# Where the causal mask is added to the query-major scores: matmul, or VectorE together with the row maximum

## The reference

```
def _L1_attn_ref(x, Wq, Wk, Wv, Wo):
    ...
    att = jnp.einsum('bqhd,bkhd->bhqk', q, k) * SCALE
    mask = _band_mask(T)
    att = jnp.where(mask[None, None, :, :], -jnp.inf, att)
    att = jax.nn.softmax(att, axis=-1)
    out = jnp.einsum('bhqk,bkhd->bqhd', att, v).reshape(B, T, C)
    return jnp.einsum('btc,oc->bto', out, Wo)
```

## Time and profile before

| | |
|---|---|
| median of three runs | 2169.51 us |
| the profiled execution's own time | 2157.45 us |
| its span, first to last instruction | 2155.7 us |
| mean granted TensorE clock | 0.875 of full speed |
| TensorE busy | 1617.6 us (75%), 10136 matmuls |
| VectorE busy | 1274.6 us (59%), 3878 instructions |
| ScalarE busy | 807.2 us (37%) |
| GpSimd busy | 510.8 us (24%) |

### The profile page before, as it was taken

One profiled execution on the slowest core, in us unless ns is written; L12 is line 12 of the kernel. 1 busy time (PEld: TensorE's weight loads), 2 busy tenths in 40 slices (PEclk: granted clock), 3 DMA queues, 4 the chain that ended last, 5 costly groups with the idle time before them and its releaser, 6 DMA issues.

```text
span 2155.7 us, 35078 instructions
## 1 busy us (share of the span) xinstructions
PE 1617.6 (75%) x10136; PEld 908.6 (42%) x10136; DVE 1274.6 (59%) x3878; ACT 807.2 (37%) x1562; POOL 510.8 (24%) x481
## 2 busy tenths in 40 slices
PE   3779888887979797979797979797998831166771
PEld 2345444444444444444444444343544421145551
DVE  5456857575858484848485757576773547721113
ACT  1225252525344443434343435252534322323322
POOL 2321212121202121212121212112120020038884
PEclk7879998999999898989898999998998665588886
DMA  5032240304040403040404031313123000025457
GB/s 143 21 44 42 25 61 10 63 7 68 4 69 7 64 7 64 14 56 15 55 22 48 25 46 30 41 33 38 35 31 56 17 6 0 0 59 99 88 88 170
DMA packets 121515, 95.40 MB, mean 44 GB/s; under 512 B 13120, under 2 KB 115904, under 8 KB 121408
## 3 DMA queue, kind: packets, MB, share of 16 engines
q1 hardware_dynamic: 110144, 85.29, 22.3%
q0 software_dynamic: 11264, 9.05, 3.4%
HBM read 63.34 MB, written 30.18 MB: 43 GB/s over the span
## 4 chain that ended last, share of the span: by engine, by line
PE 38%; issue 26%; DVE 15%; POOL 6%; DMA 6%; ACT 3%; SPq 2%; DVEq 1%; POOLq 0%; ACTq 0%
PE bo L835 5%; PE ba L576 5%; PE fa L665 4%; PE ba L581 4%; PE fa L681 4%; POOL sum_rows L543 3%; PE facc L691 3%; SPq L333 2%; PE ba L578 2%; PE ba L583 2%; DMA xin<-in_L_attn_x 1%; DMA KT<-qk_parts 1%; POOL got L520 1%; DMA sum_rows<-contrib,cur 1%; DVE nm L1270 1%
## 5 line engine op out<-in xcount | busy, mean ns | idle before, releaser
L581 PE MATMUL ba<-KT,QT 72*128 72x512 bf16 (+3 forms) x1024 | 263.2, 320 | 181.1 <-DVE nm L1270 128.5
L1014 ACT ACTIVATE probs<-ba 128x512 f32<-128x512 f32 x640 | 330.2, 622 | 114.1 <-PE ba L578 113.4
L459 POOL TENSOR_TENSOR hh<-th,gb 128x512 f32<-128x512 f32 x128 | 162.1, 1267 | 706.6 <-ACT gb L967 432.7
L1270 DVE TENSOR_REDUCE nm<-ba 128x1 f32<-128x512 f32 x256 | 174.1, 680 | 182.5 <-issue 134.3
L576 PE MATMUL ba<-QT,KT 75*128 75x512 bf16 (+3 forms) x1024 | 252.6, 310 | 34.8 <-ACT probs L1014 28.8
L581 PEld LDWEIGHTS ba<-KT,QT 72*128 72x128 bf16 x1024 | 104.9, 102 | 343.8 <-DVE nm L1270 153.2
L583 PE MATMUL ba<-mask_q,identb 128*128 128x128 bf16 x1024 | 201.3, 230 | 0.0
L578 PE MATMUL ba<-mask_k,identb 128*128 128x128 bf16 x1024 | 195.7, 224 | 0.0
L665 PE MATMUL fa<-f_nT,w 128*128 128x512 f32 x320 | 186.8, 667 | 2.4 <-ACT sc L1048 1.2
L681 PE MATMUL fa<-f_nT,w 128*128 128x512 f32 x320 | 180.0, 645 | 0.0
L983 ACT ACTIVATE sil<-fa 128x512 f32<-128x512 f32 x160 | 95.1, 594 | 217.1 <-PE fa L665 217.0
(11 more groups left out here) (283 smaller groups left out, 2731.7 us busy)
## 6 DMA issues: line engine op xcount, KB each, us to landing
QT<-qk_parts SPq DMA_DIRECT2D x288, 64.0 KB
KT<-qk_parts SPq DMA_DIRECT2D x288, 64.0 KB
qk_parts<-qkp SPq DMA_DIRECT2D x32, 384.0 KB, 2.5
fc<-in_L_ffn_fc_weight SPq DMA_DIRECT2D x32, 256.0 KB, 3.2
xn_rows<-row SPq DMA_DIRECT2D x16, 288.0 KB, 2.5
sum_rows<-zrow SPq DMA_DIRECT2D x1, 4224.0 KB, 22.0
sums<-sum_rows SPq DMA_DIRECT2D x4, 1056.0 KB, 10.4
xin<-in_L_attn_x SPq DMA_DIRECT2D x16, 256.0 KB, 14.0
```

The source lines that it names most:

```text
L459: pool.tensor_tensor(hh[:, e % 2], th[:, e % 2], gb[:, e % 2], ALU.mult).then_inc(S["s_h"], 1)
L581: pe.matmul(bank[:, col:col + w], lhsT=QT[0:QK_ROWS, head, blk * P:(blk + 1) * P], rhs=KT[0:QK_ROWS, head, 0:w], start=True, stop=False)
L1014: act.activation(probs[:, pair % 3, f_], ba[n % 3][:], ACT.Exp, scale=SCALE).then_inc(S["s_exp"], 1)
L1270: last = dve.tensor_reduce(nm[:, 3, h:h + 1], bank[:], X, ALU.max, negate=True)
```

## The change

The query-major scores keep their own matmul and lose the one with the mask. `mask_q` becomes a 128x512 tile, zero but for the triangle in its last 128 columns, so that its last w columns are the mask of a block of w columns. VectorE's reductions become `tensor_tensor_reduce`: it writes (scores + mask) times -1 back to the PSUM bank and gives the minimum over the row, which is the negated maximum. The instruction has one accumulator per partition, so the fill that one reduction covered now takes two, each of 256 columns. A nop now takes the wait for the fill. Nothing reads the values written back. The key-major side keeps its mask matmuls.

```diff
@@ the constants @@
-        mask_q = sb("mask_q", [P, P], BF16)
+        mask_q = sb("mask_q", [P, SEQ], BF16)
...
             const(pool.memset(mask_q[:], 0.0))
-            const(pool.affine_select(mask_q[:], mask_q[:], [[-1, P]], ALU.is_ge, MASKED, base=0, channel_multiplier=1))
+            last_ = mask_q[:, SEQ - P:]
+            const(pool.affine_select(last_, last_, [[-1, P]], ALU.is_ge, MASKED, base=0, channel_multiplier=1))
@@ scores @@
                     w = (blk + 1) * P
-                    pe.matmul(bank[:, col:col + w], lhsT=QT[0:QK_ROWS, head, blk * P:(blk + 1) * P],
-                              rhs=KT[0:QK_ROWS, head, 0:w], start=True, stop=False)
-                    last = pe.matmul(bank[:, col + w - P:col + w], lhsT=identb[:], rhs=mask_q[:], start=False, stop=True)
+                    last = pe.matmul(bank[:, col:col + w], lhsT=QT[0:QK_ROWS, head, blk * P:(blk + 1) * P],
+                                     rhs=KT[0:QK_ROWS, head, 0:w], start=True, stop=True)
@@ maxima @@
                 dve.wait_ge(S["s_S"], FILLS * b + n + 1)
+                apart(dve)
+
+                def lowest(head, blk, col):
+
+                    w = (blk + 1) * P
+                    return dve.tensor_tensor_reduce(bank[:, col:col + w], bank[:, col:col + w], mask_q[:, SEQ - w:], -1.0, -MASKED, ALU.add, ALU.min,
+                                                    nm[:, blk, head:head + 1])
+
                 if f in (0, 2):
-                    last = dve.tensor_reduce(nm[:, 3, h:h + 1], bank[:], X, ALU.max, negate=True)
+                    last = lowest(h, 3, 0)
                 elif f in (1, 3):
-                    dve.tensor_reduce(nm[:, 2, h:h + 1], bank[:, 0:384], X, ALU.max, negate=True)
-                    last = dve.tensor_reduce(nm[:, 0, h:h + 1], bank[:, 384:512], X, ALU.max, negate=True)
+                    lowest(h, 2, 0)
+                    last = lowest(h, 0, 384)
                 else:
-                    last = dve.tensor_reduce(nm[:, 1, h:h + 2], bank[:].rearrange("p (h k) -> p h k", h=2), X, ALU.max, negate=True)
+                    lowest(h, 1, 0)
+                    last = lowest(h + 1, 1, 256)
                 last.then_inc(S["s_red"], 1)
```

## The result

The changed kernel is slower: 2193.8 us (median of four runs, 2193.4 to 2195.7) against 2169.5 (four runs on the same chip, 2167.3 to 2172.9). The ratio is 1.0112, 95% interval 1.0095 to 1.013. The forecast was 2143 us, a gain of 27 us where 24 were lost. The time lies inside the range of 2126 to 2212.

The account below looks back on a forecast made before the run. TensorE was taken to bound the x stage's first part, VectorE its second. Per sequence -1.8 us in the first and 0 in the second; over fifteen sequences -27 us, from 2169.5 to 2143 us, range 2126 to 2212.

Parts of the forecast that it names:

- x = 0: VectorE's x stage: a fused pass with its accumulator read costs no more than the reduction it replaces; bounds -0.06 to 0.16 us.
- my own formula: Total change for an extra price x per pass: 15 x (-1.8 + 36x + what 28x exceeds 1.8 by) + 64x us.
- the bullet on writing back to PSUM: VectorE's fused passes: writing the sums to the PSUM bank was taken to cost nothing, with twice the time per element as other end.
- the half rate: Fused passes writing PSUM take twice the time per element: about +290 us, 2460 us; chance within 0.14 shared with non-overlapping passes.
- the split: Eight more VectorE passes per sequence at 0.064 us, 0.5 us, half in each part; +0.25 us on the second part's path.
- Rival 3: Gain hidden: x near 0.045, or TensorE and VectorE wait for each other in the first part; 2165 to 2174 us, chance 0.13.
- What it waits for the change does not touch, so I leave it as it is: The 134.3 us of "issue" stops at the loop's head, before the first fill is reduced, were taken as unchanged.
- rival 5: Loop's head takes longer with 72 more instructions in VectorE's body; each us there 13 us in all; no chance, put into width.
- The mask's price: TensorE, first part: 27 mask matmuls removed, 0.06 us each at full clock, 0.10 at half clock, 1.8 us per sequence.
- the nops in the stage: 40 nops per sequence before VectorE's passes, dispatched while a pass runs; without that cover, a cost within the range of x.
- The last sequence's dependence on x: Last sequence, without expert matmuls: 0.5 us more passes against short waits counted 0; a price x per pass adds 64x.
- x = 0.045: Extra price per fused pass over the reduction, in us, at which the total change is zero and above which the kernel gets slower.

Follow-up runs that it names:

- `a_no_mask`: The changed kernel with the reductions of before instead of the fused passes and no nops, so only mask matmuls are gone; 2150.7 against 2165.1 us, 0.9938.
- `w_to_sbuf`: The changed kernel with the fused passes' sums written to SBUF (an idle slice of probs) instead of back into the PSUM bank; ratio 1.0047 to before.

## Why the prediction was wrong

Three terms of the sum failed, and no single one turns the sign. In the traces they are worth 22, 17 and 18 us: -27 becomes +30, beside the 36 and 28 us of the two pairs of traces and the 24 us of the medians.

- **"x = 0" was wrong by 0.036 us a pass.** By my own formula that is 22 us, and would still have left a gain of 5. I argued from the read, and there I was right for the rows I had: the read overlaps. The fault is in the bullet on writing back to PSUM: "One element is read and one written per step in L1525 as well, so I take nothing." L1525 writes SBUF. No row of before had VectorE write PSUM, so the cost was bounded from that side by the half rate alone, and I took the near end. The output in the bank costs 0.025 us of the 0.036, as some 38 ns for each pass that starts together with a read. Per round the 0.036 are 1.28 us in the second part, and with the split 1.47.
- **Rival 3 is half true.** The first part gained 0.4 us and not 1.8, which makes 17 us over the twelve rounds. The matmuls removed were worth 1.1 there (`a_no_mask`). The fused passes took back 0.7 (19.38 to 20.04), although by my sum 1.8 us of VectorE's waits were left to absorb them; with the cheaper passes of `w_to_sbuf` they took back 0.2 (19.60). Both engines are nearly always busy in that part now (18.94 and 17.47 of 20.04 us), and each waits for the other: in the round shown VectorE still waits 2.3 us for scores, and TensorE's weight loads wait 1.5 us for VectorE, where it was 0.5. My formula let VectorE's time count only when all its waits were used up; it counts before that. Whether more than three banks would have helped, no run tells.
- **"What it waits for the change does not touch, so I leave it as it is" was wrong:** 1.48 us in each of 12 stops, 18 us of the profile's 36. I had it as rival 5, without a chance of its own, for the width. The change adds 112 instructions to VectorE's body (40 nops, 8 passes, 64 reads; I counted 72, without the nops). The same number of memsets alone gave 1.05 us per stop. Of the timed 24 us the stops' share isn't settled: with the next input held back the stops differed by 0.54 us and the loss was the same.
- **The mask's price.** 0.06 us per matmul is near: over the 27 of the first part, for which I had 1.8 us in all, it came out at 1.4 us at full clock, and at 1.1 with the clock granted lower (0.850 against 0.873).
- **Right:** the split (0.19 for 0.25), the nops in the stage, and the memset at the start. The last sequence's dependence on x isn't confirmed: it took 3.3 us more where 64x and the split's 0.5 give 2.8 at 0.036, but with the sums in SBUF it took 4.2 more, and four profiles of before without any change to this stretch run from 29.9 to 32.4 us. The point from which it gets slower, x = 0.045, was wrong: at 0.036, below it, the kernel is slower.

The Trainium skill, "VectorE: DVE Perf Modes", section "The DRAIN you can't avoid", says that the next instruction does not start before the pipe is empty, and in the same section that one which is not held starts earlier; the prediction took up the first of these alone. The steps agree in part: the read starts with the next pass and adds at most 0.01 us when the pass writes SBUF (0.61 against 0.60), so it does not have a drain of its own; when the pass writes PSUM the rows of pass and read are 30 and 59 ns longer and the next start is 0.04 us later behind a read, as if a write that takes longer were waited for. That is a reading of these rows; no run isolates it.

What stays open: why the stop also grows by 0.8 us when only TensorE's instructions are removed, how the changed kernel's 18 us of longer stops divide between VectorE's body and that, and where most of the loss lies in the written-out kernels, which have no stops.

## What to carry to other kernels

Count instructions added to a loop's body as a cost of their own if the profile shows "issue" before the first instruction behind the jump: here 112 of them cost about 1 us per round, and writing the loop out was worth 4.4%, more than any edit of the stage. Price an operation by its operands' memories, not by its kind: a row with SBUF output says nothing about PSUM output, and a row behind another instruction nothing about a packed run of the same one. And where two engines share a short queue and both are near full, don't subtract an engine's added work from its waits; expect the gain of one to be eaten by the other in part.

## What the runs showed of the hardware

- A fused add-and-minimum with an accumulator output starts the next pass 0.61 us later for 512 columns when it writes SBUF. When it writes PSUM it is 0.65 us directly behind a read of the accumulator and 0.61 behind another instruction; the difference of 37 or 38 ns is the same for 128 to 512 columns. The reduction takes 0.60. The accumulator read's row is 81 ns (SBUF) and 140 ns (PSUM), and lies beside the next pass in both.
- VectorE stood still for 11 us behind each jump back of a loop whose body it had to fetch while the DMA engines were about 0.6 busy; nothing names it in the profile but "issue", and the q14 packets that land in it, the last one 1.7 to 2.2 us before VectorE starts again.
- A nop that carries no wait and no signal leaves no instruction behind (112 more per round, and VectorE's 450 records of a round stayed 450); the change's 40 nops, which carry the waits for the fills, are 40 more semaphore records (84 to 124).
